# Perceiver kernel, cross attention: the weighted sums of a half slot gathered in one place of the order, with a larger ring of turned probabilities

## The reference, cut to what matters

```
q, k, v = split(x @ Wq + bq), split(ctx @ Wk + bk), split(ctx @ Wv + bv)
attn = softmax(q k^T * scale [+ mask])     # 64 queries x 1601 keys a head
x = x + (attn @ v) @ Wo + bo
```

## Time and profile before

| | before |
|---|---|
| median of 3 runs | 4137.4 us (4133.47 to 4137.56) |
| span of the profiled execution | 4138.0 us |
| PE busy | 3795.1 us (92%) |
| PE weight load busy | 3190.3 us (77%) |
| VectorE busy | 2772.8 us (67%) |
| ScalarE busy | 2147.9 us (52%) |
| POOL busy | 1597.5 us (39%) |
| transposes L486 | 6656 records, 916.5 us busy |
| weighted L531 | 13312 records, 444.5 us busy |

### The profile page before, as it was taken

How to read it: one execution, slowest core, us unless ns; L and a number is a source line. 1 busy time by engine, 2 the same in 40 slices (tenths; PEclk the granted TensorE clock), 3 DMA queues, 4 the chain that set the end, 5 groups by cost and what they waited for, 6 DMA issues and landing times. The chain is left out here.

```text
span 4138.0 us, 102353 instructions
## 1 busy us (share of the span) xinstructions
PE 3795.1 (92%) x42928; PEld 3190.3 (77%) x42928; DVE 2772.8 (67%) x7205; ACT 2147.9 (52%) x2963; POOL 1597.5 (39%) x1645
## 2 busy tenths in 40 slices
PE   7999999875999999988999999986997999999857
PEld 6888888634888888757788888864996888888646
DVE  5777777665777777743777777755446777777544
ACT  4555555454555555533445455533654555555434
POOL 4444343101323323130666655513773323322146
PEclk9999999987999999988999999986998999999978
DMA  3122123001111111001111111102542111110035
GB/s 96 50 65 57 49 63 112 24 16 43 42 34 37 41 38 33 19 30 36 65 53 53 49 60 55 34 13 74 208 147 73 40 34 41 42 34 26 13 109 174
DMA packets 125594, 235.94 MB, mean 57 GB/s; under 512 B 9920, under 2 KB 114768, under 8 KB 121296
## 3 DMA queue, kind: packets, MB, share of 16 engines
q1 hardware_dynamic: 118032, 175.58, 14.4%
q0 software_dynamic: 7104, 53.81, 3.7%
HBM read 208.39 MB, written 20.97 MB: 55 GB/s over the span
## 5 line engine op out<-in xcount | busy, mean ns | idle before, releaser
L599 ACT COPY prob_t<-ps 128x1024 f32<-128x1024 f32 x512 | 518.4, 1012 | 1162.0 <-PE ps L486 1162.0
L486 PE MATMUL ps<-c_ident,prob 128*128 128x128 f32 (+1 forms) x6656 | 916.5, 279 | 12.7 <-ACT prob L737 9.9
L486 PEld LDWEIGHTS ps<-c_ident,prob 128*128 128x128 f32 (+1 forms) x6656 | 717.5, 141 | 188.7 <-issue 157.2
L737 ACT ACTIVATE prob<-prob,nmx 128x1601 f32<-128x1601 f32 x512 | 828.7, 1625 | 1.2 <-DVE nmx L650 1.1
L502 PE MATMUL ps<-ctx,wk 128*128 128x400 f32 (+1 forms) x3072 | 691.1, 360 | 22.0 <-DVE vals L609 14.1
L516 PE MATMUL ps<-wv,ctx 128*128 128x256 f32 x4992 | 703.8, 289 | 3.1 <-DVE vals L609 3.1
L516 PEld LDWEIGHTS ps<-wv,ctx 128*128 128x128 f32 x4992 | 619.2, 186 | 10.0 <-DVE vals L609 4.0
L641 DVE CUSTOM_DVE_ANT_0 prob<-ps,mk 128x400 f32<-128x400 f32 (+2 forms) x1024 | 526.3, 570 | 112.7 <-PE ps L474 110.3
L644 DVE TENSOR_SCALAR_CACHE_REDUCE prob<-ps 128x400 f32<-128x400 f32 (+2 forms) x1024 | 526.1, 570 | 90.8 <-PE ps L474 90.6
L502 PEld LDWEIGHTS ps<-ctx,wk 128*128 128x128 f32 x3072 | 534.4, 191 | 45.4 <-DVE vals L609 28.5
L599 DVE COPY prob_t<-ps 128x1024 f32<-128x1024 f32 (+1 forms) x384 | 402.4, 1048 | 238.0 <-PE ps L486 237.7
(11 more groups left out here) (352 smaller groups left out, 4272.3 us busy)
## 6 DMA issues: line engine op xcount, KB each, us to landing
raw_ctx<-in_ctx_t SPq DMA_DIRECT2D x120, 400.0 KB, 3.3
raw_ctx<-in_ctx_t SPq DMA_DIRECT2D x60, 402.0 KB, 5.2
raw_ctx<-in_ctx_t SPq DMA_DIRECT2D x60, 399.0 KB, 3.2
mk<-in_mask_f SPq DMA_DIRECT2D x32, 400.2 KB, 5.5
mk<-in_mask_i SPq DMA_DIRECT2D x16, 800.5 KB, 4.4
sorted<-zeros SPq DMA_DIRECT2D x2, 3840.0 KB, 20.6
rows<-sorted SPq DMA_DIRECT2D x30, 256.0 KB, 3.3
done<-done SPq DMA_DIRECT2D x30, 256.0 KB, 2.5
```

Of the source, the lines that this page charges most:

```text
L486: mm = pe.transpose(ps[0:w, turn_bank(u, i) + a, r * P:(r + 1) * P], prob[u % 2][:, r, x * P:x * P + w], cst['ident'][:])
L599: copy(prob_t[0:w, ring(u, i), 0:nb, :], ps[0:w, turn_bank(u, i):turn_bank(u, i) + nb, :]).then_inc(st[sem], 1)
L737: a.activation(prob[h % 2][:, r, :], prob[h % 2][:, r, :], ACT.Exp, bias=nmx[:, r:r + 1], accum_out=den[h % 2][:, r:r + 1]).then_inc(st['e ...
```

## The change

The places of `weighted` now depend on the mode, and so does the number of groups in the ring. Without mask all seven groups of a slot are weighted at the end of step 0 of the next slot, and the ring holds eight. With the additive mask steps 0 and 1 stay at step 2, the other five go to step 0 of the next slot, and the ring holds six. With 'fill' nothing changes.

```diff
-WEIGHTED_AT = {2: (0, 1), 4: (2, 3)}
+WEIGHTED_AT = {None: ({}, 8), 'add': ({2: (0, 1)}, 6), 'fill': ({2: (0, 1), 4: (2, 3)}, 4)}
...
+    weighted_at, RING = WEIGHTED_AT[mask]
+    weighted_late = [x for x in range(STEPS) if x not in sum(weighted_at.values(), ())]
...
-    prob_t = st.tile("prob_t", [P, 4, 2, 512])
+    prob_t = st.tile("prob_t", [P, RING, 2, 512])
...
     def ring(u, i):
-        return (u * STEPS + i) % 4
+        return (u * STEPS + i) % RING
...
-                for x in WEIGHTED_AT.get(i, ()):
+                for x in weighted_at.get(i, ()):
                     weighted(u, x)
             if u >= 1 and i == 0:
-                for x in (4, 5, 6):
+                for x in weighted_late:
                     weighted(u - 1, x)
                 spread_denominators(u - 1)
-        for x in (4, 5, 6):
+        for x in weighted_late:
             weighted(LAST, x)
...
-        if n >= 4:
-            engine.wait_ge(*st.at('pv_mm', n - 3))
+        if n >= RING:
+            engine.wait_ge(*st.at('pv_mm', n - RING + 1))
```

## The result

The changed kernel takes 4154.07 us (median of 4 runs, 4153.61 to 4159.3), the kernel before 4135.43 in the same comparison (4133.17 to 4137.56). The ratio is 1.0041 with a 95% interval of 1.0029 to 1.0053: slower by 0.41%, some 17 us. The forecast was slower by 0.53%, 4159.4 us.

A forecast was written before the change was run, and what follows sets the result against it. PE, busy 92%, was taken as the bound, its own order setting the time. Two stages without mask at +7.3 us each and the additive one at +7.4 gave +22.0 on 4137.4, or 4159.4 us; range 4141 to 4178.

The forecast's parts named there:

- The lump: Step 0: weighting grows from 40 to 104 records without mask, +1.75 us, to 72 with the additive one, +0.87.
- Step 2: No mask only: without the weighting, the next scores start sooner, gaining 0.88 us including the wait for score banks.
- Step 4: Both modes: removing 1.01 us of weighting returns 0.39 us (even), 0.44 (odd), as step 5's values wait for bank UNIT.
- POOL's stall: Odd slots: VectorE's XNT operation no longer meets POOL's subtraction, -0.50 us each in 14 of 15.
- rival B: Slower still: POOL's stall in odd slots stays, 21 us come back, 4180 us; chance 0.11.
- The slots: Regular cross-attention slots, terms summed, both changed modes: even +0.48 us, odd -0.07 us.
- A: Faster: only switch cost counts, step 5's values do not wait for bank UNIT; 4125 us; chance 0.10.
- C: No change: the new waits at step 4 come out half as long, 4141 us; chance 0.09.

The follow-up runs named there:

- E2: Kernel before, but layers without mask weight steps 0 and 1 at step 2, the rest in the next slot's step 0, ring of six; 4153.51 us, ratio 1.0038.
- E8: Kernel before, but without mask groups 0 to 3 are weighted together at the end of step 4; 4136.86 us, ratio 0.9997.
- E4: Changed kernel, but value products of step 5 write score bank 0 instead of UNIT (not 'fill'); 4105.07 us, ratio 0.992 to the kernel before.
- E5: Kernel before, but value products of step 5 write score bank 0 instead of UNIT; 4115.64 us, ratio 0.9944.
- E3: Kernel before, but POOL starts an odd slot's first context part only after VectorE's XNT operation (not 'fill'); 4115.1 us, ratio 0.9945.
- E7: Changed kernel with score bank 0 for step 5's value products and POOL's later start; 4106.49 us, ratio 0.9922 to the kernel before.
- E1: Kernel before with only the ring made larger (eight groups without mask, six with the additive one), places unchanged; ratio 0.9995.
- E6: Kernel before with score bank 0 for step 5's value products and POOL's later start; 4095.81 us, ratio 0.9896.

## Why the prediction was right, by its own steps

**The lump** (+1.75 and +0.87 us): right. W to D takes 2.86 us with 104 records (1302.95 - 1300.09) and 1.99 with 72 (E2, 1366.70 - 1364.71), against 1.12 with 40 in the slot of the earlier trace rows, whose D is this row:

```profile
1315.52 0.40 PE L541 MATMUL ps<-diag,c_pairblk 128*32 128x128 f32 x8
```

The records keep their 0.027 us in a long run.

**Step 2** (-0.88): right. K1 to S3 is 1.28 us plus 0.1 in the bank's wait. E8 has it alone, and it comes out at nothing.

**Step 4** (-0.39 even, -0.44 odd): right, and shown as the cause by three runs: in E2, which has it alone, the two stages grow by no less than in the whole change (7.0 and 6.8 us against 6.3 and 6.0). E4 gives V another bank, its wait goes, and the gathered order gains. E5 does the same in the old order, where V starts no sooner for it and odd slots gain nothing. K2 to K3 is 5.22 us in the even slot (5.60 in the earlier trace rows), 5.42 in the odd (5.90 in the earlier trace rows). The odd one is 0.04 us better than forecast: after the wait V6 follows T6 a little sooner, which I had kept as it was.

**POOL's stall** (-0.50 in 14 of 15 odd slots): right. E3 takes it away in the old order for -0.50 us a slot, and E7 shows that nothing is left of it in the new one, in the layer with the additive mask neither. There the margin is as narrow as rival B had it: in the changed kernel's first odd slots XNT starts 0.11 to 0.13 us after POOL's subtraction ends, and in E4 one XNT met it again (0.77 us, in a slot of 23.08). Without this gain the change would have cost about 21 us more.

**The slots:** even +0.48 forecast, 22.23 to 22.71 measured; odd -0.07 forecast, 22.94 to between 22.79 and 22.83, so -0.11 to -0.15. The first slots and the two last were forecast with -1.27 and +2.4 without mask, the last two with +1.65 in the additive layer; measured in the second stage -1.3 and +2.5, in the first +1.5 for the last two. Together the three stages grew by 7.2, 6.3 and 6.0 us, 19.5 against 22.0 forecast; the odd slots are most of the difference.

**The sum against the run:** the profiled spans differ by 14.4 us only, and in them the stage with 'fill', which is the same in both, by -0.4. The other 4.7 us are outside the cross attentions, where the kernel before spent 1124.9 us in its profiled execution, the changed one 1120.2, and E1, whose code there is that of before, 1118.5. It is the spread from one execution to another of the rest of the program, not an effect of the change. The ratio, 17 us, has about 2.5 us less than the stages, inside its interval.

**The rivals:** A, that V would follow without a wait, is refuted by its own row; what it says is true once the bank is another one. There the gathered order still does not win: by their ratios E4 is 0.24% slower than E6, though it saves two visits of PE a slot without mask. In its slots PE next waits for VectorE's copies to the ring and then for the exponentials, once a slot and once in every second slot; E6 has neither wait in its regular slots. That these waits are the whole difference was not tried. The Trainium skill ("TensorEngine Tiling (Array Packing)", Key Properties) says that a change of tiling mode drains the array. What rival A made of it, that fewer visits are plain gain, holds here for the busy time of W, which fell from 444.5 to 410.4 us, and not for the span. B and C did not come about. What was not tried is a gathered order in which VectorE's copies of steps 4 to 6 are shared with another engine; whether the visits saved would pay there is open.

## What to carry to other kernels

A group of matmuls that stands between a product and the next use of its bank is not only work, it is cover: before moving it, add up the other engine's chain from the product to the release. If that chain is longer than the work that stays in between, the rest of it turns into a wait. Here taking 1.01 us of PE's work out of step 4 gave back 0.39 us, and the same work at step 0 cost 0.87. Two orders that look the same in busy shares differ by what they make meet; look for operations whose duration is not that of their twins (0.81 and 0.28 us): here one wait on an engine that had time to spare was worth 23 us. And where the waits name one bank twice a slot, try an idle bank before a new order: it was worth 23 us in the old order and 49 in the gathered one, and the change of order itself cost 17.

## What was not expected of the hardware

POOL's subtraction takes 0.3 us longer for 804 elements than for 800. The groups of the changed kernel (busy us, mean ns | idle before):

```profile
L814 POOL TENSOR_TENSOR ctx<-raw_ctx,ctx 128x800 fp32r<-128x800 f32 x120 | 192.6, 1605 | 9.6
...
L814 POOL TENSOR_TENSOR ctx<-raw_ctx,ctx 128x804 fp32r<-128x804 f32 x60 | 114.6, 1910 | 4.9
```

In E3, where POOL starts after XNT, it is 1.92 us again. So the longer time of the earlier trace rows is no part of the meeting with VectorE; whether the size, the place in memory or something else beside it makes it, no run here tells apart.
